# Gated linear attention: the gate columns join the value weights, the running sums take two matmuls, PSUM banks reassigned

## The chip, the core and the metric

The kernel runs on one core of a Trainium2 chip (trn2). The metric is the device time of one execution in microseconds; the median of three runs is compared. The engines are TensorE (PE in the profile, with its weight loads as PEld), VectorE (DVE), ScalarE (ACT), GpSimd (POOL) and SyncE (SP), which here issues most of the DMAs.

## The reference

Two decoder layers over x of shape (8, 256, 256), with a context of shape (8, 120, 256). Layer 0 is softmax attention, cross attention and a quantized gated MLP. Layer 1 begins with the gated linear attention that the change touches, then has an MLP, a two-source cross attention and a coupled feed-forward net of three cycles. What matters, for one batch element with S = 256 tokens, D = 256:

```
h   = layernorm(x) * g + b
v   = h @ Wv + bv            # (S, D)
o   = sigmoid(h @ Wo + bo)   # (S, D)
i   = h @ Wi + bi            # (S, 1)  input gate, as a log
lf  = log_sigmoid(h @ Wf + bf)   # (S, 1)  forget gate, as a log
F   = cumsum(lf)             # running sum over the tokens
A[t, s] = exp(F[t] - F[s] + i[s]) for s <= t, else 0
y   = o * (A @ v) / (A @ 1 + 1e-6)
x   = x + y
```

## The kernel before

**Tiling.** The batch of 8 is worked in NI = 4 passes of NB = 2 elements. A pass has T = 4 token tiles of P = 128 tokens, TS = 2 for each element. The feature dimension of 256 is KD = 2 tiles. Each engine has its own instruction list written out by hand, with semaphores between them; the order in the functions `layer0` and `layer1` of each engine is the order on the chip. Everything in this case is fp32, and every fp32 matmul of the program is two matmul instructions in the trace. The weights of layer 1 lie in one SBUF tensor, `late`, and are loaded once in the first pass; PSUM is one tensor `PS` of 8 banks of 512 fp32 columns.

**The stretch around the change**, at the start of `layer1`, in the order of PE (L986 to L996):

- `turn_normed(h, 0)` waits for ACT's normed tiles of batch element 0 and transposes them (4 transposes, L467) into bank 0. ACT copies them into `turned_a` with the layer norm's gain (`keep_h`, L1068).
- `gates(0)` (L755): for two token tiles, 2 matmuls each of 2 columns against `wfi`, the forget and the input gate weights, into bank 6. Then `values_m(0)` (L492): 4 matmuls of 256 columns against Wv, into bank 2.
- `turn_normed(h, 1)`, the same turn for element 1. ACT produces its input by a chain of its own: after `keep_h(0)` it normalizes x for element 1 (L1084), DVE takes its statistics (L1373), POOL the root (L1825), and ACT normalizes again (L1084).
- `outputs_m(0)` (L492, Wo, bank 4), `gates(1)`, `values_m(1)` (bank 3), `outputs_m(1)` (bank 5).
- `decays`: the running sums F. First as columns: for each element three matmuls with one moving column (L771, L772, L773) into bank 7. Then as rows: two matmuls for each element (L777, L778) into banks 0 and 1.
- `attend_m` (L789): A @ [v, 1], 257 columns, into banks 2 to 5. Then `context1_values` (L635) into banks 6 and 7.

DVE and ACT in between: DVE adds the gate biases (`z_fi`, L1606), takes |z| (L1609); ACT takes exp and ln (L1233, L1235, with table loads); DVE adds the value bias for both elements (L1616), makes `log_fi` (L1620), widens the log forget gate into `lf_wide` (L1623, four instructions), and adds the output gate's bias (L1627, two instructions), for which ACT then takes tanh (L1239). PE's `decays` wait for `lf_ready`, after L1623. When the column sums are there (`fcol_done`) DVE makes `bias_t` (L1630); when a row sum is there (`frow_done`) it adds it to the causal mask (L1633), ACT takes exp (L1245), and `attend_m` follows.

Of the kernel before, what the change touches and what calls it, by code (L numbers as in the profile page):

```python
# [5 lines left out]
ALU = mybir.AluOpType  # L6
# [5 lines left out]
P = 128  # L12
# [32 lines left out]
def decoder(nc, I, out):  # L45
    x, ctx_in = I["x"], I["ctx_1024"]
    B, S, D = x.shape
# [15 lines left out]
    G3 = I["L1_ffn_cn_w3"].shape[1]  # L63
    CYCLES = 3
    NC = NB * M
    W0 = 1.0 / (DH0 * DH0 * H)

    with ExitStack() as es:
        def sb(name, shape, dt=F32):
            return es.enter_context(nc.sbuf_tensor(name, shape, dt))  # L70

        def signal(name, per=1):
            return Signal(es.enter_context(nc.semaphore(name)), per)
# [13 lines left out]
        def bank(n):  # L87
            return PS[:, n, :]
# [39 lines left out]

        late = sb("late", [P, 8192])
        m_w = {n: view(late, 512 * i, P, [KD, D]) for i, n in enumerate(("Wv", "Wo"))}  # L130
        w1 = view(late, 1024, P, [KD, F1])
        w2 = view(late, 2560, P, [C1, D])
        c_w = {n: view(late, 4096 + 512 * i, P, [KD, D]) for i, n in enumerate(("Wq", "Wk1", "Wk2", "Wv1", "Wv2", "Wo"))}
        n_w1 = view(late, 7168, P, [KD, D])
        n_w2 = view(late, 7680, P, [KD, G2])
        g_w1 = view(late, 7936, P, [KD, G2])
        wfi = sb("wfi", [P, KD, 2])
        n_w3 = sb("n_w3", [P, G3])
# [219 lines left out]
        om_done, om_biased, om_kept = signal("om_done", TS), signal("om_biased", TS), signal("om_kept", TS)  # L358
        fi_done = signal("fi_done", NB)
        fi_exp, fi_ln = signal_rounds("fi_act_steps", ("exp", "ln"))  # L360
# [36 lines left out]
        def by_tile(w, k):  # L397
            return w.rearrange("(k p) n -> p k n", k=k)
# [18 lines left out]
        def _(sp):  # L417
# [15 lines left out]
            for n in ("Wk1", "Wk2", "Wv1", "Wv2"):  # L433
                sp.dma_start(c_w[n][:, :, :], by_tile(I["L1_xattn_" + n], KD)).then_inc(got["ctx"].sem, 16)
            for n in ("Wv", "Wo"):
                sp.dma_start(m_w[n][:, :, :], by_tile(I["L1_attn_" + n], KD)).then_inc(got["attn1"].sem, 16)
            sp.dma_start(w1[:, :, :], by_tile(I["L1_attn_W1"], KD)).then_inc(got["attn1"].sem, 16)
            sp.dma_start(w2[:, :, :], by_tile(I["L1_attn_W2"], C1)).then_inc(got["attn1"].sem, 16)
            for e, n in enumerate(("Wf", "Wi")):
                for k in range(KD):  # L440
                    sp.dma_start(wfi[:, k, e:e + 1], I["L1_attn_" + n][k * P:(k + 1) * P, :]).then_inc(got["attn1"].sem, 16)
            for n in ("Wq", "Wo"):
# [18 lines left out]
        def _(pe):  # L461
# [288 lines left out]

            def gates(it, b):
                pe.wait_ge(kept["h"].sem, kept["h"].at(it, b + 1))
                for t in range(TS * b, TS * b + TS):
                    for k in range(KD):
                        mm = pe.matmul(bank(6)[:, 2 * t:2 * t + 2], turned_a[:, k, t * P:(t + 1) * P], wfi[:, k, :],  # L755
                                       start=(k == 0), stop=(k == KD - 1))
                mm.then_inc(fi_done.sem, 1)

            def values_m(it, b):
                pe.wait_ge(hid_done.sem, hid_done.at(it, T))  # L760
                project_batch(it, turned_a, m_w["Wv"], KD, b, 2 + b).then_inc(vm_done.sem, 1)

            def outputs_m(it, b):
                project_batch(it, turned_a, m_w["Wo"], KD, b, 4 + b).then_inc(om_done.sem, 1)

            def decays(it):

                pe.wait_ge(lf_ready.sem, lf_ready.at(it, 1))
                for b in range(NB):
                    pe.wait_ge(fi_log.sem, fi_log.at(it, 1))  # L770
                    pe.matmul(bank(7)[:, 2 * b:2 * b + 1], upto[:, 0:P], log_fi[:, TS * b, 0:1], start=True, stop=True)  # L771
                    pe.matmul(bank(7)[:, 2 * b + 1:2 * b + 2], ones[:, :], log_fi[:, TS * b, 0:1], start=True, stop=False)  # L772
                    mm = pe.matmul(bank(7)[:, 2 * b + 1:2 * b + 2], upto[:, 0:P], log_fi[:, TS * b + 1, 0:1],  # L773
                                   start=False, stop=True)
                mm.then_inc(fcol_done.sem, 1)
                for b in range(NB):
                    pe.matmul(bank(b)[:, 0:S], lf_wide[:, TS * b, :], upto[:, :], start=True, stop=False)  # L777
                    pe.matmul(bank(b)[:, P:S], lf_wide[:, TS * b + 1, :], upto[:, 0:P], start=False, stop=True  # L778
                              ).then_inc(frow_done.sem, 1)

            def attend_m(it):
                pe.wait_ge(vm_kept.sem, vm_kept.at(it, NB))
                for b in range(NB):
                    if b == 1:
                        pe.wait_ge(om_biased.sem, om_biased.at(it, NB))
                    pe.wait_ge(decay_done.sem, decay_done.at(it, b + 1))
                    for st in range(TS):
                        for tt in range(st + 1):
                            mm = pe.matmul(bank(2 + TS * b + st)[:, 0:D + 1], decay[:, b, tt, st * P:(st + 1) * P],  # L789
                                           vm[:, TS * b + tt, :], start=(tt == 0), stop=(tt == st))  # L790
                        mm.then_inc(am_done.sem, 1)
# [194 lines left out]
            def layer1(it, then=None):  # L986
                turn_normed(it, "h", xs["h"], 0)
                gates(it, 0)
                values_m(it, 0)
                turn_normed(it, "h", xs["h"], 1)  # L990
                outputs_m(it, 0)
                gates(it, 1)
                values_m(it, 1)
                outputs_m(it, 1)
                decays(it)
# [373 lines left out]
        def _(dve):  # L1369
# [22 lines left out]
            def halfbank(first, hf):  # L1392
                return bank(first + hf).rearrange("p (t d) -> p t d", t=2)
# [209 lines left out]
            def layer1(it, then=None):  # L1603

                dve.wait_ge(fi_done.sem, fi_done.at(it, NB))
                dve.tensor_tensor(z_fi[:, :, :], bank(6)[:, 0:2 * T].rearrange("p (t e) -> p t e", e=2),  # L1606
                                  bfi[:, :].unsqueeze(1).to_broadcast([P, T, 2]), ALU.add).then_inc(fi_z.sem, 1)
# [6 lines left out]
                for hf in range(TS):  # L1614
                    dve.wait_ge(vm_done.sem, vm_done.at(it, hf + 1))
                    dve.tensor_tensor(vm[:, 2 * hf:2 * hf + 2, 0:D], halfbank(2, hf), broad(row["L1_attn_bv"]), ALU.add  # L1616
                                      ).then_inc(vm_kept.sem, 1)
# [7 lines left out]
                for hf in range(TS):  # L1625
                    dve.wait_ge(om_done.sem, om_done.at(it, hf + 1))
                    dve.tensor_tensor(pair(om, hf), halfbank(4, hf), broad(row["L1_attn_bo"]), ALU.add).then_inc(om_biased.sem, 1)  # L1627

                dve.wait_ge(fcol_done.sem, fcol_done.at(it, 1))
                dve.tensor_tensor(bias_t[:, :], log_fi[:, :, 1], bank(7)[:, 0:T], ALU.subtract).then_inc(bias_ready.sem, 1)  # L1630
                for b in range(NB):
# [351 lines left out]
```

## Time and profile before

| what | value |
|---|---|
| median of 3 runs | 1438.53 us (lowest 1438.09) |
| the profiled execution, first to last instruction | 1436.6 us |
| PE busy | 1223.8 us |
| DVE busy | 774.0 us |
| ACT busy | 739.3 us |
| POOL busy | 402.6 us |
| mean granted TensorE clock | 0.957 |

One of the three runs took 6541.06 us; the median leaves it out. The profiled execution is 1.9 us shorter than the median of the runs, which count a little more at both ends. The page shows busy times by engine, 40 equal slices of the span, DMA queues, the chain of work that ended last and the costliest groups of instructions. "PEclk" is the TensorE clock that was granted, as a share of 2.4 GHz: 1.00 is 2.4 GHz and 0.50 is 1.2 GHz.

### The profile page before, as it was taken

How to read it: one execution, taken by the hardware profiler on the slowest of the kernel's cores; microseconds unless marked ns; L12 is line 12 of the kernel's file. 1: busy time of each engine (PE TensorE's matmuls, PEld its weight loads, DVE VectorE, ACT ScalarE, POOL GpSimd, SP SyncE). 2: the span in 40 equal slices, each digit the busy share in tenths (PEclk: the TensorE clock that was granted, in tenths of full speed). 3: DMA queues.
4: the chain of work that ended last, by engine and by line, in shares of the span. 5: the costliest groups of instructions: out<-in, count | busy, mean ns of one | idle time of the engine just before them, and what ended most of it. 6: DMA issues, size and time to landing. Idle time of an engine off the chain costs nothing.

```text
span 1436.6 us, 19689 instructions
## 1 busy us (share of the span) xinstructions
PE 1223.8 (85%) x6274; PEld 799.9 (56%) x6282; DVE 774.0 (54%) x1901; ACT 739.3 (51%) x1882; POOL 402.6 (28%) x944
## 2 busy tenths in 40 slices
PE   6997876998899986799889987699989998679955
PEld 2454544775645644676555564477554555467644
DVE  2664376565265368546435537655535535854642
ACT  1545346575465345557446534556546544555733
POOL 1232400542033420253113341144203342015420
PEclk9999998999999999999989999899999999989966
DMA  9101300000000000000000000000000000000000
GB/s 246 55 1 50 91 1 0 1 1 0 1 1 16 1 22 1 3 0 1 1 0 16 1 22 1 2 1 1 0 1 1 16 1 1 1 1 1 1 0 15
DMA packets 27897, 20.78 MB, mean 14 GB/s; under 512 B 14412, under 2 KB 27148, under 8 KB 27660
## 3 DMA queue, kind: packets, MB, share of 16 engines
q1 hardware_dynamic: 27196, 17.83, 4.8%
q10 hardware_dynamic: 592, 1.59, 0.3%
q8 instruction: 56, 0.92, 0.3%
q14 instruction: 53, 0.43, 0.1%
HBM read 17.32 MB, written 2.10 MB: 14 GB/s over the span
## 4 chain that ended last, share of the span: by engine, by line
PE 67%; DVE 14%; ACT 9%; issue 6%; POOL 3%; DMA 1%; ACTq 0%; SPq 0%; POOLq 0%; DVEq 0%
PE PS L492 7%; PE PS L567 7%; PE PS L556 7%; PE PS L830 7%; PE PS L479 6%; PE PS L544 4%; PE PS L578 4%; PE PS L594 4%; PE PS L609 4%; PE PS L804 3%; PE PS L695 2%; PE PS L467 2%; PE PS L672 2%; PE PS L842 1%; PE PS L681 1%
## 5 line engine op out<-in xcount | busy, mean ns | idle before, releaser
L1825 POOL TENSOR_TENSOR rstd<-var,minus_half 128x2 f32<-128x2 f32 x80 | 56.4, 705 | 510.4 <-DVE nmean L1383 510.4
L1113 ACT ACTIVATE work<-PS,nmax 128x256 f32<-128x256 f32 x256 | 117.9, 473 | 85.1 <-DVE nmax L1438 85.0
L1820 POOL TENSOR_TENSOR pool_pause<-minus_half 128x1 f32<-128x1 f32 x96 | 18.7, 195 | 480.3 <-DVE inv L1445 396.4
L1291 ACT ACTIVATE work<-PS,nmax 120x256 f32<-120x256 f32 x256 | 118.4, 483 | 24.7 <-DVE nmax L1700 24.5
L567 PE MATMUL PS<-k,work 128*128 128x512 f32 x256 | 122.9, 603 | 5.7 <-ACT work L1113 2.6
L1438 DVE TENSOR_REDUCE nmax<-PS 128x2 f32<-128x512 f32 x128 | 87.2, 688 | 74.6 <-PE PS L567 74.6
L830 PE MATMUL PS<-work 128*120 128x256 f32 x512 | 119.7, 384 | 3.9 <-ACT work L1076 3.9
L1839 POOL TENSOR_SCALAR work<-work,inv 128x256 f32<-128x256 f32 x256 | 118.3, 482 | 0.0
L1700 DVE TENSOR_REDUCE nmax<-PS 120x2 f32<-120x512 f32 x128 | 86.4, 687 | 53.2 <-PE PS L830 48.6
L830 PEld LDWEIGHTS PS<-work 128*120 128x120 f32 x512 | 90.8, 183 | 29.8 <-issue 12.9
L1879 POOL TENSOR_SCALAR work<-work,head_mask 128x120 f32<-128x120 f32 x256 | 107.4, 442 | 0.0
L1084 ACT ACTIVATE x_room<-res,nshift,rstd 128x256 f32<-128x256 f32 x96 | 52.4, 594 | 100.7 <-POOL nshift L1827 100.5
L1449 DVE COPY work<-PS 128x512 f32<-128x512 f32 x64 | 44.3, 692 | 93.1 <-PE PS L578 92.6
L479 PE MATMUL PS<-turned_a,late 128*128 128x256 f32 x256 | 74.8, 454 | 2.8 <-ACT turned_a L1065 2.7
L578 PE MATMUL PS<-ident,work 128*128 128x128 f32 x512 | 69.7, 279 | 6.0 <-POOL work L1839 6.0
L594 PE MATMUL PS<-work 128*64 128x256 f32 x512 | 69.4, 391 | 6.0 <-ACT work L1119 3.1
L578 PEld LDWEIGHTS PS<-ident,work 128*128 128x128 f32 x512 | 55.4, 141 | 31.5 <-issue 17.5
L1119 ACT COPY work<-PS 128x512 f32<-128x512 f32 x64 | 37.5, 586 | 68.5 <-PE PS L578 68.5
L567 PEld LDWEIGHTS PS<-k,work 128*128 128x128 f32 x256 | 44.8, 192 | 42.4 <-issue 34.8
L479 PEld LDWEIGHTS PS<-turned_a,late 128*128 128x128 f32 x256 | 59.3, 238 | 14.8 <-ACT turned_a L1065 4.4
L544 PE MATMUL PS<-wv,x_room 128*128 128x512 f32 x128 | 58.6, 613 | 7.9 <-DMA wv<-in_L_attn_kernel_dram 7.1
L594 PEld LDWEIGHTS PS<-work 128*64 128x64 f32 x512 | 31.7, 136 | 59.3 <-issue 42.9
(254 smaller groups left out, 2555.0 us busy)
## 6 DMA issues: line engine op xcount, KB each, us to landing
xa<-in_x_dram SPq DMA_DIRECT2D x4, 512.0 KB, 3.8
out_dram<-x_room SPq DMA_DIRECT2D x4, 512.0 KB, 3.0
rows<-in_rows_dram ACTq DMA_DIRECT2D x1, 1536.0 KB, 8.4
late<-in_L_attn_W_dram SPq DMA_DIRECT2D x2, 768.0 KB, 7.9
wv<-in_L_attn_kernel_dram SPq DMA_DIRECT2D x2, 512.0 KB, 9.2
wq<-in_L_attn_kernel_dram SPq DMA_DIRECT2D x2, 512.0 KB, 9.7
wk<-in_L_attn_kernel_dram SPq DMA_DIRECT2D x2, 512.0 KB, 8.1
wo<-in_L_attn_WO_dram SPq DMA_DIRECT2D x2, 512.0 KB, 8.7
```

The lines of the kernel that those rows point to most:

```text
L479: mm = pe.matmul(bank(n)[:, c * S:(c + 1) * S], weight[:, k, c * P:(c + 1) * P], src[:, k, b * S:(b + 1) * S], start=(k == 0), stop=(k == ...
L492: mm = pe.matmul(bank(n)[:, (t % 2) * width:(t % 2 + 1) * width], lhs[:, k, t * P:(t + 1) * P], weight[:, k, :], start=(k == 0), stop=(k = ...
L544: mm = pe.matmul(bank(6 + n % 2), turned_x[:, k, t * P:(t + 1) * P], wv0[:, k, h * 512:(h + 1) * 512], start=(k == 0), stop=(k == KD - 1))
L556: mm = pe.matmul(bank(kind), w[:, k, j * P:(j + 1) * P], turned_x[:, k, :], start=(k == 0), stop=(k == KD - 1))
L567: pe.matmul(bank(2 + st), q0[:, j % 2, b * S + st * P:b * S + (st + 1) * P], k0[:, j % 2, b, :, :], start=True, stop=True).then_inc(s0_don ...
L578: mm = pe.transpose(bank(4 + hh)[:, tt * S + st * P:tt * S + (st + 1) * P], e0[:, u % 2, st, hh, tt * P:(tt + 1) * P], ident[:, :])
L594: mm = pe.matmul(bank(6)[hh * DH0:(hh + 1) * DH0, b * S:(b + 1) * S], v0[:, TS * b + tt, (2 * j + hh) * DH0:(2 * j + hh + 1) * DH0], e0t[: ...
L830: mm = pe.matmul(bank(4 + n % 4)[0:M, kv * S:(kv + 1) * S], k1m[:, g % 2, kv, 2 * r + par, :], q1[:, c, b * S:(b + 1) * S], start=True, st ...
L1113: op = act.activation(e0[:, u % 2, st, hh, :], bank(2 + st)[:, hh * S:(hh + 1) * S], ACT.Exp, bias=nmax0[:, u % 2, st, hh:hh + 1], accum_o ...
L1291: op = act.activation(e1[:, par, r, kv, :], bank(4 + n % 4)[0:M, kv * S:(kv + 1) * S], ACT.Exp, bias=nmax1[:, par, r, kv:kv + 1], accum_ou ...
L1839: op = pool.tensor_scalar(e0[:, u % 2, st, hh, :], e0[:, u % 2, st, hh, :], inv0[:, u % 2, st, hh:hh + 1], 1.0, ALU.mult, ALU.mult)
L1879: op = pool.tensor_scalar(k1m[:, g % 2, kv, h, :], k1[:, kv, c, b * M:(b + 1) * M], head_mask16[:, h:h + 1], 1.0, ALU.mult, ALU.mult)
```

## The change

- The two gate weight columns are loaded behind the 256 columns of Wv in one SBUF view `wv_fi` of 258 columns for each feature tile. `gates` is gone. `values_m` is a matmul of 258 columns for each token tile and feature tile, and each token tile has a bank of its own (2 to 5).
- `outputs_m` moves: both calls stand behind `values_m(1)`, in banks 6 and 7.
- `decays` makes the column sums of all four token tiles with two matmuls (4 and 2 columns) in bank 2 from column 384, in the place of six.
- DVE reads the gates from banks 2 to 5 once both `values_m` are done, and no longer waits for the values on their own; `attend_m` no longer waits for `om_biased`.
- Two weight views of the feed-forward net (`n_w2`, `g_w1`) move to the front of `late`.

```diff
-        late = sb("late", [P, 8192])
-        m_w = {n: view(late, 512 * i, P, [KD, D]) for i, n in enumerate(("Wv", "Wo"))}
+        late = sb("late", [P, 8192 + KD * (D + 2) - 512])
+        wv_fi = view(late, 7680, P, [KD, D + 2])
+        m_w = {"Wo": view(late, 512, P, [KD, D])}
...
-                    sp.dma_start(wfi[:, k, e:e + 1], I["L1_attn_" + n][k * P:(k + 1) * P, :]).then_inc(got["attn1"].sem, 16)
+                    sp.dma_start(wv_fi[:, k, D + e:D + e + 1], I["L1_attn_" + n][k * P:(k + 1) * P, :]).then_inc(got["attn1"].sem, 16)
...
-            def gates(it, b):
+            def values_m(it, b):
+
                 pe.wait_ge(kept["h"].sem, kept["h"].at(it, b + 1))
+                pe.wait_ge(hid_done.sem, hid_done.at(it, T))
                 for t in range(TS * b, TS * b + TS):
                     for k in range(KD):
-                        mm = pe.matmul(bank(6)[:, 2 * t:2 * t + 2], turned_a[:, k, t * P:(t + 1) * P], wfi[:, k, :],
+                        mm = pe.matmul(bank(2 + t)[:, 0:D + 2], turned_a[:, k, t * P:(t + 1) * P], wv_fi[:, k, :],
                                        start=(k == 0), stop=(k == KD - 1))
-                mm.then_inc(fi_done.sem, 1)
-
-            def values_m(it, b):
-                pe.wait_ge(hid_done.sem, hid_done.at(it, T))
-                project_batch(it, turned_a, m_w["Wv"], KD, b, 2 + b).then_inc(vm_done.sem, 1)
+                mm.then_inc(vm_done.sem, 1)
 
             def outputs_m(it, b):
-                project_batch(it, turned_a, m_w["Wo"], KD, b, 4 + b).then_inc(om_done.sem, 1)
+                project_batch(it, turned_a, m_w["Wo"], KD, b, 6 + b).then_inc(om_done.sem, 1)
...
                 pe.wait_ge(lf_ready.sem, lf_ready.at(it, 1))
-                for b in range(NB):
-                    pe.wait_ge(fi_log.sem, fi_log.at(it, 1))
-                    pe.matmul(bank(7)[:, 2 * b:2 * b + 1], upto[:, 0:P], log_fi[:, TS * b, 0:1], start=True, stop=True)
-                    pe.matmul(bank(7)[:, 2 * b + 1:2 * b + 2], ones[:, :], log_fi[:, TS * b, 0:1], start=True, stop=False)
-                    mm = pe.matmul(bank(7)[:, 2 * b + 1:2 * b + 2], upto[:, 0:P], log_fi[:, TS * b + 1, 0:1],
-                                   start=False, stop=True)
+                pe.wait_ge(fi_log.sem, fi_log.at(it, 1))
+                pe.matmul(bank(2)[:, CUM:CUM + T], upto[:, 0:P], log_fi[:, :, 0], start=True, stop=False)
+                mm = pe.matmul(bank(2)[:, CUM + 1:CUM + T:TS], ones[:, :], log_fi[:, 0:T:TS, 0], start=False, stop=True)
                 mm.then_inc(fcol_done.sem, 1)
...
-                    if b == 1:
-                        pe.wait_ge(om_biased.sem, om_biased.at(it, NB))
...
                 turn_normed(it, "h", xs["h"], 0)
-                gates(it, 0)
                 values_m(it, 0)
                 turn_normed(it, "h", xs["h"], 1)
-                outputs_m(it, 0)
-                gates(it, 1)
                 values_m(it, 1)
-                outputs_m(it, 1)
+                for b in range(NB):
+                    outputs_m(it, b)
                 decays(it)
...
-                dve.wait_ge(fi_done.sem, fi_done.at(it, NB))
-                dve.tensor_tensor(z_fi[:, :, :], bank(6)[:, 0:2 * T].rearrange("p (t e) -> p t e", e=2),
+                dve.wait_ge(vm_done.sem, vm_done.at(it, NB))
+                dve.tensor_tensor(z_fi[:, :, :], PS[:, 2:2 + T, D:D + 2],
```

## Rows read from the trace of the kernel before

**Rows 1.** The page: busy by engine (us, share, instructions), and its chain by engine
```profile
PE 1223.8 (85%) x6274; PEld 799.9 (56%) x6282; DVE 774.0 (54%) x1901; ACT 739.3 (51%) x1882; POOL 402.6 (28%) x944
PE 67%; DVE 14%; ACT 9%; issue 6%; POOL 3%; DMA 1%; ACTq 0%; SPq 0%; POOLq 0%; DVEq 0%
```

**Rows 2.** The chain that ended last, second pass: start us, us, what
```profile
583.46 1.87 PE PS L755 x8
585.33 3.47 PE PS L492 x8
588.79 0.44 PE PS L467 x4
589.23 1.73 PE PS L492 x8
590.96 0.79 PE PS L755 x8
591.74 3.56 PE PS L492 x16
...
595.42 0.38 PE PS L771 x2
...
596.69 0.22 PE PS L773 x2
596.91 0.54 PE PS L777 x2
597.46 0.23 PE PS L778 x2
597.71 0.70 DVE work L1633
```

**Rows 3.** The timeline, second pass: start us, us, engine, line, [idle before]
```profile
582.38 1.02 ACT L1068 ACTIVATE turned_a<-PS,cols 128x256 f32<-128x256 f32 x2 [1.01 <-PE PS L467]
...
586.80 1.09 ACT L1084 ACTIVATE xh_room<-x_room,nshift,rstd 128x256 f32<-128x256 f32 x2 [2.42 <-POOL nshift L1827]
...
591.78 0.17 DVE L1606 TENSOR_TENSOR z_fi<-PS,scalars 128x8 f32<-128x8 f32 x1 [6.06 <-PE PS L755]
...
592.28 0.69 DVE L1616 TENSOR_TENSOR work<-PS,rows 128x512 f32<-128x512 f32 x1
...
593.62 0.69 DVE L1616 TENSOR_TENSOR work<-PS,rows 128x512 f32<-128x512 f32 x1 [0.64 <-PE PS L492]
593.71 0.21 ACT L1235 ACTIVATE zl_fi<-zl_fi 128x8 f32<-128x8 f32 x1
...
594.22 0.16 DVE L1620 TENSOR_TENSOR log_fi<-z_fi,zl_fi 128x8 f32<-128x8 f32 x1
...
595.20 1.28 DVE L1627 TENSOR_TENSOR work<-PS,rows 128x512 f32<-128x512 f32 x2
...
596.95 0.16 DVE L1630 TENSOR_TENSOR bias_t<-log_fi,PS 128x4 f32<-128x4 f32 x1 [0.47 <-PE PS L773]
```

**Rows 4.** PE by stretch: us, PE busy (instructions), granted clock, DMA share, GB/s
```profile
239.30:241.50 2.20, 1.12 (x4) 0.50 0.00 0
241.50:246.80 5.30, 5.26 (x16) 0.50 0.00 0
246.80:250.10 3.30, 3.30 (x22) 0.94 0.00 0
...
583.40:588.50 5.10, 5.04 (x16) 0.50 0.01 3
588.50:591.70 3.20, 3.20 (x23) 1.00 0.02 5
...
1382.30:1385.50 3.20, 1.95 (x8) 0.50 0.00 0
1385.50:1390.60 5.10, 5.10 (x14) 0.50 0.00 0
```

**Rows 5.** Line 441, the gate weights' loads: ns min/median/max, first and last start
```profile
L441 SPq DMA_DIRECT2D wfi<-in_L_attn_Wi_dram x2: 680/873/1066, 142.4 to 143.5; - x2
```

More of the change, by code:

```diff
@@ L64, in decoder @@
     CYCLES = 3
+    CUM = 384
     NC = NB * M
@@ L134, in decoder @@
         n_w1 = view(late, 7168, P, [KD, D])
-        n_w2 = view(late, 7680, P, [KD, G2])
-        g_w1 = view(late, 7936, P, [KD, G2])
-        wfi = sb("wfi", [P, KD, 2])
+        n_w2 = view(late, 0, P, [KD, G2])
+        g_w1 = view(late, 256, P, [KD, G2])
         n_w3 = sb("n_w3", [P, G3])
@@ L358, in decoder @@
         om_done, om_biased, om_kept = signal("om_done", TS), signal("om_biased", TS), signal("om_kept", TS)
-        fi_done = signal("fi_done", NB)
         fi_exp, fi_ln = signal_rounds("fi_act_steps", ("exp", "ln"))
@@ L434, in _ @@
                 sp.dma_start(c_w[n][:, :, :], by_tile(I["L1_xattn_" + n], KD)).then_inc(got["ctx"].sem, 16)
-            for n in ("Wv", "Wo"):
-                sp.dma_start(m_w[n][:, :, :], by_tile(I["L1_attn_" + n], KD)).then_inc(got["attn1"].sem, 16)
+            sp.dma_start(wv_fi[:, :, 0:D], by_tile(I["L1_attn_Wv"], KD)).then_inc(got["attn1"].sem, 16)
+            sp.dma_start(m_w["Wo"][:, :, :], by_tile(I["L1_attn_Wo"], KD)).then_inc(got["attn1"].sem, 16)
             sp.dma_start(w1[:, :, :], by_tile(I["L1_attn_W1"], KD)).then_inc(got["attn1"].sem, 16)
@@ L1614, in layer1 @@
                 for hf in range(TS):
-                    dve.wait_ge(vm_done.sem, vm_done.at(it, hf + 1))
-                    dve.tensor_tensor(vm[:, 2 * hf:2 * hf + 2, 0:D], halfbank(2, hf), broad(row["L1_attn_bv"]), ALU.add
+                    dve.tensor_tensor(vm[:, 2 * hf:2 * hf + 2, 0:D], PS[:, 2 + 2 * hf:4 + 2 * hf, 0:D], broad(row["L1_attn_bv"]), ALU.add
                                       ).then_inc(vm_kept.sem, 1)
@@ L1626, in layer1 @@
                     dve.wait_ge(om_done.sem, om_done.at(it, hf + 1))
-                    dve.tensor_tensor(pair(om, hf), halfbank(4, hf), broad(row["L1_attn_bo"]), ALU.add).then_inc(om_biased.sem, 1)
+                    dve.tensor_tensor(pair(om, hf), halfbank(6, hf), broad(row["L1_attn_bo"]), ALU.add).then_inc(om_biased.sem, 1)
                 dve.wait_ge(fcol_done.sem, fcol_done.at(it, 1))
-                dve.tensor_tensor(bias_t[:, :], log_fi[:, :, 1], bank(7)[:, 0:T], ALU.subtract).then_inc(bias_ready.sem, 1)
+                dve.tensor_tensor(bias_t[:, :], log_fi[:, :, 1], bank(2)[:, CUM:CUM + T], ALU.subtract).then_inc(bias_ready.sem, 1)
                 for b in range(NB):
```

## The prediction

> **What bounds the kernel now.** I read the page first: PE is busy 85% of the span and holds 67% of the chain that ended last, with DVE, ACT and POOL as links between its stretches [rows 1]. The kernel is bound by PE and by hand-overs between engines, and PE's time is worth its full length only where the chain runs through it. So I read the chain in the second of the four passes [rows 2]. It goes through PE without a break from 583.46 to 595.30: gates(0), values(0), the turn of element 1, outputs(0), gates(1), values(1), outputs(1). Then come the running sums from 595.42, and at 597.71 DVE's first mask addition (L1633). I take that start as the end of the changed stretch: whatever moves it moves the rest of the pass, since ACT's exp and the attention follow at once.
>
> Next the timeline of DVE and ACT in the same stretch [rows 3], to see what is nearly late. The log forget gate (L1620) starts at 594.22 and the first running sum at 595.42, 1.20 us later; PE was done with the outputs at 595.30 [rows 2]. Both paths, PE's own work and the gate chain through DVE and ACT, end within about 0.1 us of each other. Shortening one alone gains nothing.
>
> Last the granted clock by stretch [rows 4]. The 1.87 us of gates(0) against the 0.79 us of gates(1), and the 3.47 us of values(0) against the 1.73 us of outputs(0) [rows 2], are the same work at the two levels of the clock, 1.2 and 2.4 GHz. PE enters this stretch after idle time, at the low level. In the second pass the clock is back at 588.50, right when the turn of element 1 begins; in the first, where the work starts at 239.3, the stretch from 246.80 has 0.94 on average, so it came back near 247.2, 7.9 us after the start.
>
> **The change, part by part** (second pass; the others are alike).
>
> *gates(0) goes.* 1.87 us less on PE [rows 2]. values(0) starts at 583.46 and takes 3.47 us at the low clock (2 columns more on 256 are 0.03 us): it ends at 586.96. But the turn of element 1 needs ACT's normed tiles, which end at 586.80 + 1.09 = 587.89 [rows 3], by a chain that starts behind `keep_h(0)` and has no PE in it. It does not move. So the turn starts at 587.93: of 1.87 us, 0.86 us are gained and PE idles for 1.0 us, where it did not idle before.
>
> *outputs(0) moves behind values(1).* It was the cover for ACT's copy of the turned tiles. That copy takes 1.02 us [rows 3], with 0.09 us for the two hand-overs. PE now idles for it: values(1) cannot start before the turn's end + 1.1 us. The turn takes 1.12 us at the low clock [rows 4] or 0.44 us at the full one [rows 2], so values(1) starts at 590.15 or at 589.5.
>
> *gates(1) goes, and the gates come with values(1).* 0.79 us less. z_fi (L1606), at 591.78 before, now waits for the last value matmul: 590.15 + 1.75 = 591.9 at the full clock, or 590.15 + 3.5 = 593.65 at the low one.
>
> *The gate chain.* From z_fi to the end of ACT's ln it was 593.92 - 591.78 = 2.14 us [rows 3]; the log forget gate follows at z + 2.2. Before, it came at z + 2.44, because DVE's second value bias (L1616) waited 0.64 us for values(1); now both stand ready and are over at z + 1.8, under the ln. Then 1.20 us to the first running sum as before: z + 3.4. With the full clock from values(1) on that is 595.35; the outputs, 16 instructions in 3.46 us (twice the 1.73 us), end at 595.4. So the sums start at 595.4, where they started before: one path is given back by the idles, the other by the later gates.
>
> *Running sums.* Six matmuls took 0.38 + 5 x 0.22 = 1.49 us; two take 0.38 + 0.22 = 0.60 us, since one-column matmuls cost a fixed 0.22 us, and 4 columns will not cost more than the gates' two-column ones, 0.79 / 4 = 0.20 us each [rows 2]. That is 0.89 us gained on the path: the row sums need 0.54 + 0.23 us more, and L1633 can start 1.40 us after the first sum, where it was 2.29 us. Does DVE follow? Its output biases (L1627) end 595.20 + 1.28 = 596.48, `bias_t` then takes 0.16 us, against 595.42 + 1.40 = 596.82: ready 0.15 us early. So the whole 0.89 us counts, and little more would.
>
> *Costed at nothing.* The four gate loads land near 143 us [rows 5], 100 us before the first reader at 241.5. DVE's reads have the same shapes. The `om_biased` wait dropped from `attend_m` was always over, since DVE makes the biases ahead of L1633, and ACT's exp waits for that. Banks 6 and 7 are free because the normed tiles of element 1 come out of them; `context1_values` stands behind the same exp. Nothing in SP's or POOL's queue is passed. If this cover were gone the price would be one 0.69 us bias.
>
> *The clock.* This is the term the trace of before can only bound. Before, the turn of element 0 was followed by one 1.1 us idle and then by work with no hole until the clock was back. After, there are three holes of about 1 us each between 581.4 and 590.2. Elsewhere in this trace the clock took longer where holes came: from 1382.3 PE was busy 1.95 of 3.2 us, and the clock stayed at 0.50 to 1390.6, 8.3 us after the start and 5.1 us into unbroken work [rows 4]; in the second pass it came back after 5.04 us of nearly unbroken work. Unbroken work now begins only with values(1) at 590.15. If it takes 5.1 to 5.7 us again, the clock is back at about 595.6: values(1) ends at 593.65, the outputs then have 1.95 us at the low clock (4.5 of 16 instructions at 0.43 us), and the other 11.5 take 11.5 x 0.216 = 2.5 us, to 598.1. The sums start 2.7 us late; less 0.89 us, the pass loses 1.8 us. If the clock is back at the end of values(1), gates and outputs both give 597.1: +1.7 - 0.9 = +0.8 us. If it is full from values(1) on: -0.9 us. If full from the turn on: another 0.5 us earlier, -1.4 us. The bounds are thus -1.4 and +1.8 us a pass. The trace's passes returned at slightly different points, so I expect a mixture; the three holes speak for late. I take two passes at +1.8, one at +0.8 and one at -1.4: +3.0 us.
>
> The Trainium skill, "TensorE: Matmul & The Clock Gate", in its section on a second HAM failure mode, says that short idles between groups of matmuls can be enough to make the clock gate swing between its two states. The rows agree in that the clock stayed low over a stretch with holes; by that rule every pass would be late (4 x 1.8 = +7.2 us), where the rows alone leave the mixture (+3.0 us).
>
> **Sum.** 1436.6 + 3.0 = 1439.6 us of span; with the 1.9 us between span and median of before, 1441.5 us.
>
> **The rivals.**
>
> *A, the clock comes back late in all four passes.* Decides if PE is still at 0.50 when values(1) ends, everywhere. 1438.5 + 7.2 = 1445.7 us, slower. For it: the new holes at 586.96 and at the copy. Against: the clock was back 7.1 us after the start in one pass before, and that would be 588.5 again if its return only needs work up to there. Chance 0.17.
>
> *B, the clock is not disturbed.* The change then gives what it removes: 4 x 0.9 = 3.6 us up to 4 x 1.4 = 5.6 us, 1433 to 1435 us, faster. For it: the work from 583.46 to 586.96 stays. Chance 0.2.
>
> *C, no net change,* because the gate chain and not PE sets the start, or because returns of both kinds cancel: 1437.5 to 1439.5 us. For it: the two paths end within 0.1 us. Chance 0.13.
>
> *D, the low clock holds past the sums,* into the attention and `context1_values`. The rest of the outputs, 11.5 instructions, would cost 2.5 us more and the sums about as much as they save: over 4 us a pass beyond the forecast's late one, above 1455 us. Against: that is 8 us of unbroken work, and no stretch of the rows shows it. Chance 0.04.
>
> **How the numbers follow.** The forecast (a mixture of late and undisturbed passes, 1439.5 to 1444.5 us) has 0.46 and is the likeliest; its value is 1441.5 us. The range takes in C, most of A and the near part of B: 1434 to 1446.5 us. Two per cent is 28.8 us, about what a measurement of this kernel can tell from no change; no case but a much worse D comes near it. So within 2%: 0.97; faster by more: 0.01; slower by more: 0.02.
>
> **What would show each step.** No L755 rows, 8 instructions of 258 columns for each value stage, and PE idle about 1 us ahead of the second turn and again ahead of values(1). z_fi directly behind the last value matmul, and the log forget gate 2.2 us behind it. Two pairs of column-sum rows, 0.6 us in all, and L1633 1.4 us after the first. The granted clock at 0.50 past the start of values(1) in some passes; for those the outputs take over 5 us for their 16 instructions. The prediction is wrong if the clock returns in all passes before values(1), if the wait for ACT's normed tiles is absent, or if DVE's biases delay L1633 beyond 1.5 us after the first sum.

## The result and the profile after

The changed kernel takes 1448.51 us (median; 1447.82 to 1449.33) against 1439.65 us for the kernel before on the same chip: a ratio of 1.0063, 95% interval 1.005 to 1.0076. The 1439.65 us are the median of four runs, one of them the 6541.06 us run; the median of the other three is 1438.53 us. So the change makes the kernel slower by 9 to 10 us, clear of the interval and well within two per cent. 1441.5 us was forecast, in a range that ended at 1446.5 us.

The page of the changed kernel, busy time by engine and the chain by engine, beside [rows 1]:

```profile
PE 1226.7 (85%) x6178; PEld 796.5 (55%) x6186; DVE 773.4 (53%) x1901; ACT 738.5 (51%) x1882; POOL 400.8 (28%) x944
PE 65%; DVE 14%; ACT 9%; issue 6%; POOL 3%; DMA 1%; ACTq 0%; SPq 0%; POOLq 0%; DVEq 0%
```

PE has 96 instructions fewer and is busy 2.9 us longer: its instructions were slower on average. The mean granted clock went from 0.957 to 0.944.

The timeline of the second pass, PE with the instructions of ACT and DVE that it hangs on (start us, duration us, engine, line, instruction, idle time before it). Lines moved: L757 is `values_m`, L768 and L769 are the column sums, L772 and L773 the row sums, L1623 the mask addition.

```profile
585.43 1.11 PE L467 MATMUL PS<-ident,xh_room 128*128 128x128 f32 x4 [3.85 <-ACT xh_room L1075]
587.73 3.80 PE L757 MATMUL PS<-late,turned_a 128*128 128x258 f32 x8 [1.19 <-ACT turned_a L1059]
591.00 1.09 ACT L1075 ACTIVATE xh_room<-x_room,nshift,rstd 128x256 f32<-128x256 f32 x2 [2.42 <-POOL nshift L1817]
592.14 1.11 PE L467 MATMUL PS<-ident,xh_room 128*128 128x128 f32 x4 [0.61 <-ACT xh_room L1075]
594.72 3.81 PE L757 MATMUL PS<-late,turned_a 128*128 128x258 f32 x8 [1.47 <-ACT turned_a L1059]
598.32 4.19 PE L492 MATMUL PS<-late,turned_a 128*128 128x256 f32 x16
598.57 0.17 DVE L1597 TENSOR_TENSOR z_fi<-PS,scalars 128x8 f32<-128x8 f32 x1 [8.64 <-PE PS L757]
...
600.82 0.17 DVE L1610 TENSOR_TENSOR log_fi<-z_fi,zl_fi 128x8 f32<-128x8 f32 x1 [0.48 <-ACT zl_fi L1226]
...
602.35 0.28 PE L768 MATMUL PS<-log_fi,upto 128*128 128x4 f32 x2
602.49 0.36 PE L769 MATMUL PS<-log_fi,ones 128*128 128x2 f32 x2
...
603.65 1.35 DVE L1623 TENSOR_TENSOR work<-PS,causal 128x512 f32<-128x512 f32 x2 [0.34 <-PE PS L773]
```

Beside [rows 2]: the second value stage (594.72) takes 3.81 us, where half of the last 16 instructions, values(1), took 1.8 us before; PE stands idle ahead of the first value stage (1.19 us, a hole that was there before as 1.11 us), ahead of the second turn (0.61 us) and ahead of the second value stage (1.47 us). The clock by stretch, columns as in [rows 4]:

```profile
587.70:592.10 4.40, 3.80 (x8) 0.50 0.01 4
592.10:594.30 2.20, 1.11 (x4) 0.50 0.03 7
594.30:599.40 5.10, 4.68 (x11) 0.50 0.00 0
599.40:602.40 3.00, 3.00 (x16) 0.99 0.00 0
```

It came back at 599.4, 14.0 us after the first turn began; before it was 7.1 us (from 581.4 to 588.5 [rows 4]).

I measure each pass from the first turn (L467) to DVE's first mask addition, and call this the stretch. Before, it took 16.77, 16.29, 16.75 and 16.33 us; after, 18.16, 18.22, 18.49 and 18.04 us. That is +1.4, +1.9, +1.7 and +1.7 us, 6.8 us together. The spans of the two profiled executions differ by 10.9 us, so 4.2 us were lost outside the stretch, in code that the change does not touch. One place is PE's out_1 (L492) in layer 1's cross attention, first pass; after, then before, from the two timelines:

```profile
336.89 3.54 PE L492 MATMUL PS<-late,turned_a 128*128 128x256 f32 x8 [0.79 <-ACT turned_a L1059]
```

```profile
334.39 1.99 PE L492 MATMUL PS<-late,turned_a 128*128 128x256 f32 x8 [0.80 <-ACT turned_a L1068]
```

The same 8 instructions cost 1.55 us more, and the clock by stretch shows why (after, then before):

```profile
333.20:336.60 3.40, 1.66 (x20) 1.00 0.00 0
336.60:340.10 3.50, 3.21 (x8) 0.51 0.02 5
```

```profile
330.70:334.10 3.40, 1.65 (x20) 1.00 0.00 0
334.10:337.50 3.40, 3.11 (x20) 1.00 0.00 0
```

PE had been busy the same half of the time ahead of it in both kernels. In the one the clock fell, in the other it did not. The same fall stands in the third and the fourth pass of the changed kernel, and not in the second.

### The profile page after: what moved, and what is told of

Its sections match the earlier page's. It is cut to its first block, busy times and chain, and to the rows that moved or that the text cites. A ratio compares the mean times of both kernels' runs of the same rounds, so it can differ in the third digit from the quotient of the medians.

```text
span 1447.6 us, 19498 instructions
## 1 busy us (share of the span) xinstructions
PE 1226.7 (85%) x6178; PEld 796.5 (55%) x6186; DVE 773.4 (53%) x1901; ACT 738.5 (51%) x1882; POOL 400.8 (28%) x944
## 4 chain that ended last, share of the span: by engine, by line
PE 65%; DVE 14%; ACT 9%; issue 6%; POOL 3%; DMA 1%; ACTq 0%; SPq 0%; POOLq 0%; DVEq 0%
PE PS L567 7%; PE PS L556 7%; PE PS L823 7%; PE PS L492 6%; PE PS L479 5%; PE PS L544 4%; PE PS L578 4%; PE PS L594 4%; PE PS L609 4%; PE PS L797 3%; PE PS L695 2%; PE PS L467 2%; PE PS L672 2%; PE PS L681 1%; PE PS L835 1%
## 5 line engine op out<-in xcount | busy, mean ns | idle before, releaser
L1810 POOL TENSOR_TENSOR pool_pause<-minus_half 128x1 f32<-128x1 f32 x96 | 18.5, 193 | 480.5 <-DVE inv L1436 396.4
L578 PEld LDWEIGHTS PS<-ident,work 128*128 128x128 f32 x512 | 55.3, 141 | 31.4 <-issue 17.5
L1527 DVE TENSOR_REDUCE maxx<-PS 128x8 f32<-128x960 f32 x32 | 37.0, 1155 | 51.3 <-PE PS L672 50.8
```

The costliest lines, as they stand in the source:

```text
L578: mm = pe.transpose(bank(4 + hh)[:, tt * S + st * P:tt * S + (st + 1) * P], e0[:, u % 2, st, hh, tt * P:(tt + 1) * P], ident[:, :])
```

## The experiments

Two theories stood against each other. The **clock theory**: the holes that the change opens on PE keep the clock low until the outputs are nearly over. The **chain theory**: the later gates and the exposed copy cost the time as waits, at whatever clock. All added matmuls below have results that nobody reads.

### Filling the holes: e1_fill

```diff
                 values_m(it, 0)
+                filler(1)      # one matmul of 256 columns into bank 6
                 turn_normed(it, "h", xs["h"], 1)
+                filler(1)
                 values_m(it, 1)
```

> The changed kernel with one matmul of 256 columns added ahead of the turn of element 1 and one ahead of values_m(1), whose results nobody reads; the order, the waits and all else are those of the changed kernel. Clock theory (the holes that the change opens on PE keep the TensorE clock at 0.50 until the outputs are nearly over): the clock is back 6 to 8 us after the turn of element 0, the stretch from that turn to DVE's first mask addition goes from 18.2 us to 15 to 16 us, 9 to 12 us over four passes, so the ratio to before is 0.997 to 1.000. Rival, chain theory (the later gates and the exposed copy cost the time by themselves): the added matmuls lie in idle time and change nothing, or cost up to 0.5 us a pass: ratio 1.006 to 1.008.

Measured: 1430.63 us, ratio 0.9954 (0.9938 to 0.997). The stretch is 15.72, 16.28, 16.35 and 15.28 us. The timeline of the second pass, PE:

```profile
580.03 1.11 PE L467 MATMUL PS<-ident,xh_room 128*128 128x128 f32 x4 [3.85 <-ACT xh_room L1082]
582.33 3.80 PE L757 MATMUL PS<-late,turned_a 128*128 128x258 f32 x8 [1.19 <-ACT turned_a L1066]
585.93 1.06 PE L764 MATMUL PS<-late,turned_a 128*128 128x256 f32 x2
586.78 0.99 PE L467 MATMUL PS<-ident,xh_room 128*128 128x128 f32 x4
587.61 0.60 PE L764 MATMUL PS<-late,turned_a 128*128 128x256 f32 x2
589.40 2.01 PE L757 MATMUL PS<-late,turned_a 128*128 128x258 f32 x8 [1.20 <-ACT turned_a L1066]
```

More work made the kernel faster than the change alone, by 1.0063 - 0.9954 or some 16 us. The second value stage takes 2.01 us again. Nothing in the chain of waits was altered: the chain theory is refuted as the cause of the loss. Of the 18.6 us between the two profiled executions, 9.3 us lie in the stretches, as the clock theory had it (9 to 12 us); the other 9.3 us lie outside, where no theory had put any, and so the ratio came out below the 0.997 to 1.000 that was expected.

### Giving the cover back: e2_cover and e5_cover_fill

e2_cover is the changed kernel with outputs_m(0) back between the second turn and values_m(1).

```diff
                 turn_normed(it, "h", xs["h"], 1)
+                outputs_m(it, 0)
                 values_m(it, 1)
-                for b in range(NB):
-                    outputs_m(it, b)
+                outputs_m(it, 1)
```

> The changed kernel with outputs_m(0) moved back between the turn of element 1 and values_m(1). Clock theory: one of the two holes is filled, the clock comes back about 10 us after the turn of element 0 instead of 17, and the stretch is 15.5 to 17 us, 1.2 to 2.7 us less a pass: ratio 0.999 to 1.003. Chain theory: the gates come even later, by the length of outputs_m(0), 1.7 us, less the hole of 1.1 us: the stretch grows by 0.6 us a pass, ratio 1.007 to 1.009.

Measured: 1449.96 us, ratio 1.0077 (1.006 to 1.0094), which is the chain theory's number. But its mechanism is not there: the stretch did not grow, it shrank from 72.9 to 68.9 us over four passes. The match of the number is luck. The clock theory's numbers missed as well: the clock came back 10.5 to 11.3 us after the turn in three passes, about as expected, yet the stretch was 17.5 to 18.0 us there, and the ratio above its 0.999 to 1.003. In the first pass the clock was back 6.7 us after the turn and the stretch was 15.75 us. The rest of the loss moved behind the stretch. Timeline of PE, second pass:

```profile
595.46 1.89 PE L492 MATMUL PS<-late,turned_a 128*128 128x256 f32 x8
599.12 0.38 PE L768 MATMUL PS<-log_fi,upto 128*128 128x4 f32 x2 [1.77 <-DVE work L1613]
...
602.44 5.14 PE L782 MATMUL PS<-work 128*128 128x257 f32 x12 [0.61 <-ACT work L1236]
```

Now PE is done with the outputs before the gate chain is, and idles for 1.77 us. The clock falls at 600.3, within the row sums, and the attention (L782) takes 5.14 us where it took 2.8 us. It is 0.50 to 607.1, and the like happens in the third and the fourth pass. e5_cover_fill adds three matmuls in this hole:

```diff
                 outputs_m(it, 1)
+                filler(3)      # three matmuls of 256 columns into bank 0
                 decays(it)
```

> The kernel with outputs_m(0) back ahead of values_m(1) (the second experiment), and three matmuls of 256 columns more behind outputs_m(1), whose results nobody reads. There PE stood idle 1.77 us for the gate chain, and in three of four passes the clock then fell during the running sums, and the attention matmuls took 5.14 us. Clock theory: with that hole nearly filled the clock holds, the attention takes 2.8 us, the fall behind the sums is gone in all passes, and the total falls from ratio 1.0077 to 0.998 to 1.003. Chain theory: nothing waits for the added work, the ratio stays at 1.007 to 1.009.

Measured: 1444.88 us, ratio 1.0038 (1.0024 to 1.0052), less of a gain than was expected. The attention is back at its length, and no fall stands behind the sums in any pass:

```profile
599.54 1.46 PE L764 MATMUL PS<-late,turned_a 128*128 128x256 f32 x6
601.47 0.38 PE L773 MATMUL PS<-log_fi,upto 128*128 128x4 f32 x2 [0.47 <-DVE work L1619]
...
604.73 2.84 PE L787 MATMUL PS<-work 128*128 128x257 f32 x12 [1.24 <-ACT work L1242]
```

But the stretch is 17.7 us, since its early part is the same as e2_cover's with the first hole open, and the fall ahead of out_1 now stands in all four passes (336.5, 681.2, 1026.0 and 1370.7 us).

### The running sums alone: e3_sums

The kernel before, with the new two-matmul column sums in bank 7.

> The kernel before with the two-matmul column sums alone (in bank 7 as before). Both theories: the two matmuls take 0.6 us in the place of 1.5 us and the stretch is 0.9 us shorter in each pass, 3.6 us in all: ratio 0.997 to 0.998. If the sums are hidden behind DVE's biases: ratio 0.999 to 1.000.

Measured: 1431.28 us, ratio 0.9961 (0.9943 to 0.9978). The chain of the second pass:

```profile
595.24 0.38 PE PS L770 x2
595.62 0.22 PE PS L771 x2
595.84 0.54 PE PS L774 x2
596.38 0.23 PE PS L775 x2
596.63 0.70 DVE work L1630
```

The sums take 0.60 us as the prediction had it, and the mask addition comes 1.39 us after the first. The stretch fell by 2.9 us over four passes, where 3.6 us was expected. The kernel as a whole gained 7 us, more than the 0.997 to 0.998 that was expected: about 3.7 us came from outside the stretch, again without a change of code there. Its runs also spread: four of the six took 1430.2 to 1431.7 us, two 1436.1 and 1436.7 us. The profiled one is of the shorter group, and no trace shows what the longer ones did. e1_fill has one such run of five (1435.9 us), e7_sums_warm three of ten (1442.8 to 1443.2 us).

### The moved outputs alone: e4_moved

The kernel before, with outputs_m(0) behind values_m(1).

```diff
-                outputs_m(it, 0)
                 gates(it, 1)
                 values_m(it, 1)
+                outputs_m(it, 0)
                 outputs_m(it, 1)
```

> The kernel before with outputs_m(0) moved behind values_m(1) alone; gates, banks and six-matmul sums stay. Clock theory: a hole of 1.1 us opens ahead of gates(1), in some passes before the clock is back: the stretch grows from 16.5 to 17 to 19 us: ratio 1.001 to 1.006. Chain theory: PE idles 1.1 us and is that much later, while the gates come 0.7 us earlier: the stretch grows by 1.0 to 1.1 us a pass at whatever clock: ratio 1.003.

Measured: 1445.24 us, ratio 1.005 (1.0033 to 1.0067). The stretch is 19.05 to 19.39 us, 2.7 us more a pass, well above the chain theory's 1.1 us and a little above the clock theory's 17 to 19 us. Timeline, PE, second pass:

```profile
590.68 0.60 PE L467 MATMUL PS<-ident,xh_room 128*128 128x128 f32 x4
592.55 1.05 PE L755 MATMUL PS<-wfi,turned_a 128*128 128x2 f32 x8 [1.26 <-ACT turned_a L1068]
593.46 7.11 PE L492 MATMUL PS<-late,turned_a 128*128 128x256 f32 x24
```

The exposed copy is 1.26 us of idle. The clock had come back before it (the turn takes 0.60 us), and it fell again at 594.0: the 24 instructions take 7.11 us, where 24 x 0.216 = 5.2 us is their time at 2.4 GHz. So of 2.7 us a pass some 1.1 us are the wait itself and the rest is the clock. Both theories have their part here; moving this cover is a loss by itself. The four stretches lost 10.8 us and the kernel only some 7 us, because the time outside the stretch was 5.1 us shorter than in the kernel before.

### Warming ahead of the stretch: e6_fill_warm and e7_sums_warm

Three matmuls on constants ahead of the first turn, in e1_fill and in e3_sums.

```diff
+                warm(3)        # three matmuls of 256 columns into bank 4
                 turn_normed(it, "h", xs["h"], 0)
```

> The changed kernel with the two added matmuls of the first experiment and three more (256 columns each, on constants, unread) ahead of the turn of element 0, in PE's 4 us of idle time there. Clock theory: PE enters the stretch with less idle time behind it, the clock falls later or not at all in some passes: stretch 15 to 16 us as in the first experiment or up to 1 us less; ratio 0.992 to 0.996. Rival: the clock at the entry does not matter, since the first part waits for ACT anyway: ratio as the first experiment's, 0.995 to 0.996.

> The kernel before with the two-matmul column sums (third experiment) and three added matmuls of 256 columns ahead of the turn of element 0. If the change's gate merge is worth something by itself once the clock is cared for, this one stays behind the changed kernel with its holes filled: stretch 15.0 to 15.8 us, ratio 0.994 to 0.997, against 0.992 to 0.996 for that one. If the merge is worth nothing, both give the same within 1 us.

Measured: 1438.75 us, ratio 1.000 (0.9991 to 1.001), and 1438.21 us, ratio 1.0003 (0.999 to 1.0015). Neither expectation on the ratio came true: both kernels lost what their parents had gained. Timeline of e6_fill_warm, PE, second pass:

```profile
576.29 1.05 PE L745 MATMUL PS<-wd,work 128*128 128x256 bf16 x8 [1.10 <-ACT work L1189]
580.26 2.90 PE L769 MATMUL PS<-upto,ident 128*128 128x256 f32 x6 [2.92 <-issue]
582.95 1.06 PE L467 MATMUL PS<-ident,xh_room 128*128 128x128 f32 x4
```

The idle time that I wanted to use is not free. (L745 is layer 0's MLP, whose matmuls are bf16: only the stretch and its surroundings in layer 1 are fp32, not the whole program.) PE's list is a loop whose body starts with layer 1 of one pass and ends with layer 0 of the next, so at this place the loop goes back to its head, and PE waited 2.92 us for nothing that the profile shows before its first instruction. The added matmuls ran after that, at the low clock, and held the turn back: 5.6 us from the end of L745 to the turn, against 3.9 us in the kernel before. The same stands in the third pass (2.54 us). In the first and the last pass, which PE enters without a jump back, the added matmuls follow L745 directly and the turn is not held. That makes some 3 us of the 9.0 us by which the time outside exceeds e1_fill's. For the rest there is more low clock (66.2 against 43.2 us, in the table below), with a fall ahead of out_1 in three passes. The stretches were short, 62.4 us together against 63.9 us in e7_sums_warm. The medians of the two agree within 1 us, so the kernels as a whole showed no worth of the gate merge here, though the stretches differ by 0.4 us a pass in its favour.

### One hole or three: e8_fill_first and e9_three

e8_fill_first keeps only the first of e1_fill's two matmuls. e9_three adds a third, behind the first turn.

> The changed kernel with one added matmul only, in the hole ahead of the turn of element 1; the hole ahead of values_m(1) stays. Clock theory: this is the earlier of the two holes and the one that keeps the clock from coming back 7 us after the start; with it filled the clock is back by the end of values_m(1) in most passes: stretch 15 to 16.5 us, ratio 0.995 to 1.000. If both holes matter alike: stretch about 17 us, ratio 1.001 to 1.003.

> The changed kernel with an added matmul of 256 columns (unread) in each of its three holes: behind the turn of element 0, ahead of the turn of element 1, and ahead of values_m(1). Clock theory: PE has almost no hole from the first turn on, the clock is back as early as with the holes at the second and third place filled or earlier: stretch 14.9 to 15.9 us, ratio 0.993 to 0.996. Chain theory: as the changed kernel, 1.006.

Measured: e8_fill_first 1432.16 us, ratio 0.9956 (0.9939 to 0.9973), stretch 15.46 to 16.22 us. One matmul ahead of the second turn is nearly enough. e9_three 1430.96 us, ratio 0.9949 (0.9933 to 0.9966), stretch 15.23 to 16.22 us (14.9 to 15.9 us expected), which is e1_fill's within the intervals. In e9_three the clock came back 3.8 to 4.5 us after the turn, in e1_fill 7.1 to 7.5 us, and the stretches are the same within 0.6 us over four passes: until the second turn PE waits for ACT's normed tiles anyway, so the clock there was worth nothing. What counts is that it is back by the second value stage.

### The worth of the gate merge: e12_sums_fill

The kernel before with the new sums and one added matmul behind the first turn, to be set against e9_three.

> The kernel before with the two-matmul column sums and one added matmul (unread) in its one hole, behind the turn of element 0. Against the changed kernel with its holes filled this shows what the gate merge is worth by itself. Clock theory: stretch 15.0 to 15.8 us, ratio 0.994 to 0.997. If the merge has a worth of its own, the changed kernel with its three holes filled is ahead by 0.3 us a pass or more.

Measured: 1431.47 us, ratio 0.9953 (0.9936 to 0.997), stretch 63.2 us over four passes (15.74 to 15.88 us each) against 63.0 us of e9_three (15.39, 16.19, 16.22 and 15.23 us): 0.04 us a pass, not 0.3. First turn and mask addition, second pass, e9_three and then e12_sums_fill:

```profile
580.58 1.12 PE L467 MATMUL PS<-ident,xh_room 128*128 128x128 f32 x4 [3.86 <-ACT xh_room L1088]
596.76 1.35 DVE L1636 TENSOR_TENSOR work<-PS,causal 128x512 f32<-128x512 f32 x2 [0.27 <-PE PS L783]
```

```profile
580.22 1.11 PE L467 MATMUL PS<-ident,xh_room 128*128 128x128 f32 x4 [3.85 <-ACT xh_room L1087]
595.99 1.35 DVE L1636 TENSOR_TENSOR work<-PS,causal 128x512 f32<-128x512 f32 x2 [0.27 <-PE PS L780]
```

With the clock cared for on both sides, the merged gates with the moved outputs and the separate ones in the old order cost the same. What the merge is worth with the outputs left in place was measured with the clock back early in one pass only, the first of e2_cover: 15.75 us, against 15.6 to 16.0 us in e3_sums. So no gain of the change was seen but that of the sums. By the intervals e1, e3, e8, e9 and e12 are equal, and the simplest that beats both kernels is e3_sums, the kernel before with the new sums and nothing else.

### The same kernel again: e10_again

> The changed kernel once more, nothing altered. If the clock's falls outside the changed stretch (at 336.6, 1026.1 and 1370.9 us, just ahead of the matmuls of out_1) are chance of one execution, they stand elsewhere or are absent here; if they follow from where the pass has got to, they return within 1 us of the same places. Time 1447.5 to 1449.5 us.

Measured, in one execution: 1442.77 us, 5 us below the lowest of the four earlier runs and below the 1447.5 us expected, but still 4.7 us above the median of the kernel before on the same chip (1438.04 us) and 11.8 us above e9_three on it. The stretch is 15.39, 18.20, 18.49 and 18.05 us. The time outside, 1370.9 us, is that of the kernel before: in this execution the stretches alone make the difference. Columns as in [rows 4], from the turn of the first pass on:

```profile
241.20:247.90 6.70, 4.92 (x12) 0.51 0.00 0
247.90:251.40 3.50, 2.32 (x12) 1.00 0.00 0
251.40:256.60 5.20, 5.16 (x27) 1.00 0.00 0
```

In this execution the first pass had the clock back 6.6 us after its turn began, with the same holes. The fall ahead of out_1 was absent in the first pass (8 instructions from 334.93 in 1.99 us), and present in the third and fourth (1022.6 and 1367.4 us). These are 3.5 us earlier than before, as the passes themselves are: behind the turn they stand at 96.6 and 96.0 us, in the earlier execution at 96.5 and 96.0 us. So both of the expectation's answers hold in part: one execution's clock is no sure copy of another's, yet most falls return.

### A plain delay: e11_shift

The kernel before with four added matmuls directly ahead of the running sums.

> The kernel before with four added matmuls of 256 columns (unread) directly ahead of the running sums, 1.7 us a pass at the full clock, on the chain. If time outside the changed stretch is indifferent to when a pass reaches it, the total grows by 4 x 1.7 = 6.9 us: ratio 1.0048. If the clock's falls outside the stretch depend on it, the total differs from that by up to 5 us either way, and the time outside the stretch less half of PE's busy time at the low clock there stays within 1340 to 1344 us, as in all kernels so far.

Measured: 1445.84 us (1444.74 to 1450.11), ratio 1.005 (1.0033 to 1.0067). By the ratio this is near the plain 6.9 us (the medians differ by 7.8 us), so it doesn't tell the two answers apart. The profiled execution is 11.7 us longer than that of before, 6.8 us in the stretch and 4.9 us outside, and it is the longest of the four; the runs spread over 5.4 us. Its time outside less half of the low-clock time is 1344.6 us, just above the 1344 us of the expectation.

### Outside the stretch

For each trace I added up PE's matmul records that lie at the low clock outside the four stretches, and took half of that time (what these records would save at 2.4 GHz) off the time outside (span less stretches). Microseconds:

| kernel | span | four stretches | outside | PE busy at 0.50, outside | outside less half |
|---|---|---|---|---|---|
| before | 1436.6 | 66.1 | 1370.5 | 57.0 | 1342.0 |
| after | 1447.6 | 72.9 | 1374.7 | 63.7 | 1342.8 |
| e1_fill | 1429.0 | 63.6 | 1365.4 | 43.2 | 1343.8 |
| e2_cover | 1448.4 | 68.9 | 1379.5 | 77.0 | 1341.0 |
| e3_sums | 1430.0 | 63.2 | 1366.8 | 52.4 | 1340.6 |
| e4_moved | 1442.4 | 77.0 | 1365.4 | 43.1 | 1343.8 |
| e5_cover_fill | 1444.3 | 70.6 | 1373.7 | 58.6 | 1344.4 |
| e6_fill_warm | 1436.8 | 62.4 | 1374.4 | 66.2 | 1341.3 |
| e7_sums_warm | 1436.0 | 63.9 | 1372.1 | 56.6 | 1343.8 |
| e8_fill_first | 1429.7 | 63.7 | 1366.1 | 47.0 | 1342.6 |
| e9_three | 1429.5 | 63.0 | 1366.4 | 49.5 | 1341.6 |
| e10_again | 1441.0 | 70.1 | 1370.9 | 53.5 | 1344.1 |
| e11_shift | 1448.4 | 73.0 | 1375.4 | 61.6 | 1344.6 |
| e12_sums_fill | 1429.3 | 63.2 | 1366.1 | 47.7 | 1342.2 |

The time outside ranges over 14 us in code that is the same but for the added warm-up matmuls; without its low-clock part it ranges over 4 us. Before against after, the low clock outside cost (63.7 - 57.0) / 2, or about 3 us. The moved weight views and banks, which the changed kernel has and the kernel before has not, cost nothing outside: e9_three has them and e12_sums_fill has not, and their times outside are 1366.4 and 1366.1 us.

Inside the stretches this account does not hold: e1_fill and e9_three have nearly the same stretches (63.6 and 63.0 us) with 24.4 and 14.9 us of PE's time at the low clock in them, because work ahead of a wait for ACT costs nothing there. The experiments give it directly. With its holes filled the changed kernel's stretches take 63.0 to 63.7 us: 2.4 to 3.1 us less than before (66.1 us), about the 2.9 us of e3_sums, and 9.2 to 9.9 us less than its own 72.9 us, which is what the late clock cost.

The fall ahead of out_1 goes with the place that the pass has reached. Leaving out e6 and e7, whose added matmuls stand ahead of the turn, the traces hold 48 passes. In 14 of them out_1 began 95.7 to 96.8 us after the turn, and the clock fell ahead of it in 12. In the other 34 it began before 95.1 or after 97.3 us, and the clock never fell there. Stretches of 17.5 to 18.5 us with the attention at full clock put out_1 into that band; stretches under 17 us or over 19 us did not. This is a count over traces and no experiment, and it gives no cause; e6 and e7 have such falls at 93.2 to 94.8 us.

## Why the prediction was wrong, point by point

- **The bound, right.** PE's work and the gate chain were both on the edge, and what moved DVE's mask addition moved the pass.
- **gates(0) gone, right.** The second turn waits for ACT's normed tiles (0.61 us of idle, 1.0 us forecast). The value stage took 3.8 us where 3.5 us was forecast; the timeline of before has it at 3.61 us, so the two columns more cost 0.2 us and not 0.03 us at the low clock.
- **The moved outputs, right.** The copy is exposed: 1.1 to 1.5 us of idle, 1.1 us forecast.
- **The gate chain, right.** The log forget gate follows z_fi by 600.82 - 598.57 = 2.25 us (2.2 forecast).
- **The running sums, right.** 0.6 us, and the addition 1.30 us after the first (1.40 forecast). The margin for DVE was 596.82 - 596.64 = 0.18 us by the prediction's own numbers, not 0.15 us, and DVE waited for the row sum as forecast (0.34 us). e3_sums alone confirms the sign and most of the size (2.9 of 3.6 us in the stretches).
- **A late pass, right in size.** The forecast's late pass begins its sums 598.1 - 581.4 = 16.7 us after the turn; it was 602.35 - 585.43 = 16.9 us, and the passes lost 1.4 to 1.9 us (1.8 forecast). The clock was back 14.0 us after the turn (14.2 forecast). The outputs took 4.19 us; the prediction's own sum gives 1.95 + 2.5 = 4.45 us, and the "over 5 us" among its signs does not follow from it. The early pass had its size right too: -1.4 us forecast, 15.39 - 16.77 = -1.38 us in the first pass of e10_again. (From 590.15 to 589.5 is 0.65 us and not the 0.5 us that the forecast added.)
- **How many passes are late, wrong.** This is the first step that failed. "Two passes at +1.8, one at +0.8 and one at -1.4" made 3.0 us of what was 6.8 us: all four were late, which I had as rival A with a chance of 0.17. I took the return of the clock for something that spreads out over the passes, though the trace of before had it between 7.1 and 7.9 us in all four (two are in [rows 4]), which speaks for one answer in all four. e10_again shows that an early pass exists, one of the eight passes profiled. The Trainium skill's sentence on short idles, in "TensorE: Matmul & The Clock Gate", section "A second HAM failure mode", was on the right side: the runs agree in seven of these eight passes, 18.0 to 18.5 us with the holes and about 15.9 us with them filled. The Trainium skill tells there of a clock that swings between its states; here the holes mostly kept it low for longer, and falls behind a hole were seen in e4_moved (594.0 us) and e2_cover (600.3 us).
- **The time outside, left out.** This is the second step that failed. The prediction says of the mask addition that "whatever moves it moves the rest of the pass". That took the time behind the mask addition as fixed, and the sum had no term for it; it was 4.2 us longer. Of the 8.0 us by which the span missed the forecast (1447.6 against 1439.6 us), 3.8 us are the count of late passes and 4.2 us this. Rival A with the 4.2 us from outside gives 1445.7 + 4.2 = 1449.9 us, near the 1448.5 us measured. The falls ahead of out_1 cost 3 x 1.55 = 4.7 us, which is the whole of it. In e10_again, with two such falls, the time outside was that of before, so this term is no fixed price of the change. The trace of before could have given a warning: its four passes hold the same work, and yet the second had a time from mask addition to the next turn of 327.7 us, 2.4 us more than the 325.3 us of the first and third.
- **Rival D, not here.** It turned up in e2_cover, by the same mechanism: a hole ahead of small matmuls, and the attention at the low clock.

What stays open: why a fall stands ahead of out_1 when a pass reaches it at some times and not at others, with PE just as busy before it, and why the second pass of the changed kernel was without it in both executions. No run was made that sets this apart.

## What to carry to other kernels

Before work that covers a hand-over is removed or moved, price the hole at its length and also at the work that may then run at 1.2 GHz, and count it in every pass that looks alike, not in half of them. One unread matmul in the right hole (e8_fill_first) was worth more here than all the instructions that the change saved; but look first whether the idle time is real waiting or the loop's own turn-around, as it was at the head of PE's loop. And in a kernel whose clock falls now and then, a difference of less than 1% can come from places that the edit never touched, so compare the edited stretch by itself before believing either sign.

## What the runs showed that I had not expected

- The gain of a small saving is not its size: 0.73 us a pass saved in e3_sums, 2.9 us over four passes, became 7 us. In the delayed kernel 6.8 us added became 7.8 us by the medians and 11.7 us in the profiled execution.
- The lengths of a pass, from turn to turn, lie in two groups. In the five fastest kernels (e1, e3, e8, e9, e12) they are 341.2 to 341.8 us; in after and the other seven they are 343.2 to 347.4 us, but for the first ones of e2 (340.9) and e10 (340.7). The kernel before has 342.1, 344.0 and 342.1 us.
- Where its loop jumps back, PE stood idle for 2.92 and 2.54 us (e6_fill_warm, second and third pass) ahead of its first instruction, although that instruction waits for no semaphore; in the two passes that it enters without a jump there was no such idle time.
